# Attention in a three-attention transformer kernel: keys projected before queries, first loads over two queues, first weighings of a half one score item earlier, row group of the maxima by place in the stream

## The reference

```python
x = x + time_mix(layernorm(x))                  # 64x64 state per head, chunks of 64 tokens
x = x + ffn(layernorm(x))                       # "F"
x = x + latent_attention(layernorm(x))          # "L", causal
x = x + ffn(layernorm(x))                       # "H", the same weights as F

def ffn(x):
    h = layernorm(x, ln1_g, ln1_b)
    scores = einsum('bqhd,bkhd->bhqk', h @ Wq, h @ Wk) / sqrt(8)
    x = x + (softmax(scores) @ (h @ Wv)) @ Wo
    m = layernorm(x, ln2_g, ln2_b)
    return x + weighted sum over the 2 best of 8 experts e of gelu(m @ W1[e] + b1[e]) @ W2[e] + b2[e]
```

## Time and profile before

| | |
|---|---|
| time, median of 3 runs | 3130.23 us (3124.28 to 3133.2) |
| profiled execution: its own time | 3137.23 us |
| its span | 3134.4 us |
| PE (TensorE matmul) busy | 2739.7 us, 87% |
| DVE (VectorE) busy | 2117.2 us, 68% |
| ACT (ScalarE) busy | 1712.2 us, 55% |
| POOL (GpSimd) busy | 429.1 us, 14% |
| L543, reduction of the maxima, x2688 | 626.2 + 625.7 + 354.5 us |
| L482, exponentials, x1408 | 522.4 + 522.3 + 294.3 us |

### The profile page before, as it was taken

The page is one execution under the profiler, slowest core; times in us unless marked ns, Lnnn a source line. Parts: engine busy times, 40 slices in busy tenths (PEclk is TensorE's granted clock), DMA queues, the critical chain, the costliest instruction groups (busy, mean ns, idle before and its releaser), DMA issues. The chain is left out here.

```text
span 3134.4 us, 62592 instructions
## 1 busy us (share of the span) xinstructions
PE 2739.7 (87%) x20985; PEld 1214.1 (39%) x20985; DVE 2117.2 (68%) x4017; ACT 1712.2 (55%) x2055; POOL 429.1 (14%) x664
## 2 busy tenths in 40 slices
PE   6788857999999997999599999948998989897998
PEld 2688851223233232444244444421232323233443
DVE  5544456999989895222578777747998989894222
ACT  4222212777777775443156665633776767675433
POOL 1222202111111110000221111120111111110000
PEclk9888856999999998999699999976999999998999
DMA  1000002011100110210201111111110111011111
GB/s 44 1 0 0 0 1 87 23 36 39 39 30 30 39 39 22 82 46 34 87 27 52 53 45 54 47 57 48 39 38 21 39 39 36 23 39 35 69 60 33
DMA packets 86864, 120.25 MB, mean 38 GB/s; under 512 B 16261, under 2 KB 59231, under 8 KB 84223
## 3 DMA queue, kind: packets, MB, share of 16 engines
q1 hardware_dynamic: 83401, 114.80, 11.7%
q10 hardware_dynamic: 3248, 2.21, 0.3%
HBM read 83.40 MB, written 20.55 MB: 33 GB/s over the span
## 5 line engine op out<-in xcount | busy, mean ns | idle before, releaser
L543 DVE TENSOR_REDUCE Hmaxes<-Hm 128x1 f32<-128x512 f32 x1024 | 626.2, 684 | 77.0 <-PE Hm L425 77.0
L543 DVE TENSOR_REDUCE Fmaxes<-Fm 128x1 f32<-128x512 f32 x1024 | 625.7, 684 | 66.1 <-PE Fm L425 66.1
L482 ACT ACTIVATE Hprob<-Hs 128x1024 f32<-128x1024 f32 x512 | 522.4, 1026 | 173.1 <-PE Hs L386 138.8
L482 ACT ACTIVATE Fprob<-Fs 128x1024 f32<-128x1024 f32 x512 | 522.3, 1026 | 161.0 <-PE Fs L386 126.2
L543 DVE TENSOR_REDUCE Lmaxes<-Lm 128x1 f32<-128x512 f32 (+3 forms) x640 | 354.5, 606 | 108.4 <-PE Lm L371 54.5
L482 ACT ACTIVATE Lprob<-Ls 128x1024 f32<-128x1024 f32 (+7 forms) x384 | 294.3, 778 | 177.6 <-PE Ls L386 99.5
L425 PE MATMUL Hm<-Hka,Hqa 60*128 60x512 bf16 x1024 | 299.0, 407 | 66.5 <-DVE Hmaxes L543 32.0
L425 PE MATMUL Fm<-Fka,Fqa 60*128 60x512 bf16 x1024 | 298.9, 406 | 54.3 <-DVE Fmaxes L543 30.5
L404 PE MATMUL Ho<-Hprob,Hvh 128*32 128x256 f32 x4096 | 320.4, 397 | 0.3 <-ACT Hprob L482 0.3
L404 PE MATMUL Fo<-Fprob,Fvh 128*32 128x256 f32 x4096 | 319.9, 396 | 0.3 <-ACT Fprob L482 0.3
L386 PE MATMUL Fs<-Fqa,Fka 60*128 60x512 bf16 x1024 | 248.1, 389 | 1.7 <-ACT Fprob L482 1.7
(11 more groups left out here) (430 smaller groups left out, 3290.2 us busy)
## 6 DMA issues: line engine op xcount, KB each, us to landing
FEwb<-FE_weights SPq DMA_DIRECT2D x8, 1024.0 KB, 5.2
HEwb<-HE_weights SPq DMA_DIRECT2D x8, 1024.0 KB, 5.6
Fvh<-Fvstack SPq DMA_DIRECT2D x17, 256.0 KB
Lvh<-Lvstack SPq DMA_DIRECT2D x17, 256.0 KB
Hvh<-Hvstack SPq DMA_DIRECT2D x17, 256.0 KB
FEw<-in_L_ffn_W SPq DMA_DIRECT2D x16, 256.0 KB, 2.9
HEw<-in_L_ffn_W SPq DMA_DIRECT2D x16, 256.0 KB, 2.8
Fqa<-F_qparts SPq DMA_DIRECT2D x34, 96.0 KB
```

What stands on the lines that cost most here:

```text
L482: nc.scalar.activation(prob[:, :, :].rearrange("p k q -> p (k q)")[:, lo:hi], sps[n % 2][:, o:o + hi - lo], ACT.Exp, scale=SCALE).then_inc ...
L543: nc.vector.reduce_max(maxes[:, a, t, half:half + 1], src[:, 0:w], AX.X).then_inc(max_free, 1)
```

## The change

There are four edits, all in `attention`, and so in F, L and H alike.

1. **Order of the projections.** Keys come first, then queries, then values. The split is interleaved: ScalarE takes the high part of the next piece before the middle part of this one, VectorE subtracts for the next piece before it finishes this one, with three `rest` tiles instead of two.
2. **First loads.** SP stores k and loads `ka` of head 0. ScalarE's queue stores q. `qa` of head 0 is loaded after that, row group 0 by SP and row group 1 by ScalarE's queue. `vh` has a semaphore of its own, `v_loaded`, and is loaded at the start of the second block, as is everything of head 1. One of the two fills of `ka` with minus ones goes from GpSimd to VectorE, ahead of its first subtraction.
3. **`KEPT_BACK`** is 3 instead of 4.
4. **Row group of a maxima matmul**: the parity of its place in the stream of maxima and turns (`PLACE`), not that of its block of keys.

```diff
+    v_loaded = [semaphore(nc, heads, f"{name}v_loaded{s}") for s in range(SLOTS)]
+    vh = heads.enter_context(nc.sbuf_tensor(name + "vh", [P, SLOTS, NT * VW], F32))
+    LOADS = 16 * GROUPS * (2 * PARTS + 1)
...
+    def load_v(engine, h, s):
+        engine.dma_start(vh[:, s, :], vstack[:, bass.ds(h, 1), :, :].rearrange("p h t d -> p (h t d)"))\
+            .then_inc(v_loaded[s], 16)
...
-        QK = [(w, b) for w in range(2) for b in range(NB)]
+        KQ = [(w, b) for w in (1, 0) for b in range(NB)]
...
-                for n, (w, b) in enumerate(QK):
-                    cols = slice(b * BANK, (b + 1) * BANK)
+                def take_high(n):
+                    w, b = KQ[n]
                     act.wait_ge(projected, n + 1)
-                    nc.scalar.activation(parts[:, w, 0, cols], ps[n % 4][:, :], ACT.Copy).then_inc(first, 1)
+                    nc.scalar.activation(parts[:, w, 0, b * BANK:(b + 1) * BANK], ps[n % 4][:, :], ACT.Copy)\
+                        .then_inc(high, 1)
+
+                take_high(0)
+                for n, (w, b) in enumerate(KQ):
+                    if n + 1 < len(KQ):
+                        take_high(n + 1)
                     act.wait_ge(second, n + 1)
-                    nc.scalar.activation(parts[:, w, 1, cols], rest[:, n % 2, :], ACT.Copy).then_inc(first, 1)
+                    nc.scalar.activation(parts[:, w, 1, b * BANK:(b + 1) * BANK], rest[:, n % 3, :], ACT.Copy)\
+                        .then_inc(middle, 1)
+                    if n == NB + 2:
+                        act.wait_ge(split, NB + 2)
+                        store(act, 0, 0, q_stored)
+                act.wait_ge(split, 2 * NB)
+                store(act, 0, 1, q_stored)
                 act.wait_ge(ones, 1)
                 for b in range(NB):
-                    act.wait_ge(projected, len(QK) + b + 1)
+                    act.wait_ge(projected, len(KQ) + b + 1)
 
                     nc.scalar.activation(
                         vstack[:, 0:NH, 4 * b:4 * b + 4, 0:DH].rearrange("p h t d -> p t h d"),
-                        ps[(len(QK) + b) % 4][:, :].rearrange("p (t h d) -> p t h d", t=4, h=NH),
+                        ps[(len(KQ) + b) % 4][:, :].rearrange("p (t h d) -> p t h d", t=4, h=NH),
                         ACT.Copy).then_inc(v_read, 1)
+                act.wait_ge(q_stored, 32)
+                load_q(act, 0, 0, groups=(1,))
+                act.wait_ge(v_read, NB)
 
...
-                for r in range(GROUPS):
-                    nc.gpsimd.memset(ka[64 * r:64 * r + 32, :, :], -1.0).then_inc(filled, 1)
-                pool.wait_ge(filled, 2)
+                nc.gpsimd.memset(ka[0:32, :, :], -1.0).then_inc(filled, 1)
+                pool.wait_ge(filled, 1)
                 nc.gpsimd.memset(vstack[:, :, :, :], 1.0).then_inc(ones, 1)
                 nc.gpsimd.memset(topp[:, :, :, :], 0.0).then_inc(filled, 1)
...
-                for n, (w, b) in enumerate(QK):
+                def take_second(n):
+                    w, b = KQ[n]
+                    dve.wait_ge(high, n + 1)
+                    if n >= 3:
+                        dve.wait_ge(split, n - 2)
+                    nc.vector.tensor_tensor(rest[:, n % 3, :], ps[n % 4][:, :], parts[:, w, 0, b * BANK:(b + 1) * BANK],
+                                            ALU.subtract).then_inc(second, 1)
+
+                nc.vector.memset(ka[64:96, :, :], -1.0).then_inc(minus_ones, 1)
+                take_second(0)
+                for n, (w, b) in enumerate(KQ):
                     cols = slice(b * BANK, (b + 1) * BANK)
-                    dve.wait_ge(first, 2 * n + 1)
-                    nc.vector.tensor_tensor(rest[:, n % 2, :], ps[n % 4][:, :], parts[:, w, 0, cols],
-                                            ALU.subtract).then_inc(second, 1)
-                    dve.wait_ge(first, 2 * n + 2)
-                    nc.vector.tensor_tensor(parts[:, w, 2, cols], rest[:, n % 2, :], parts[:, w, 1, cols],
+                    if n + 1 < len(KQ):
+                        take_second(n + 1)
+                    dve.wait_ge(middle, n + 1)
+                    nc.vector.tensor_tensor(parts[:, w, 2, cols], rest[:, n % 3, :], parts[:, w, 1, cols],
                                             ALU.subtract).then_inc(split, 1)
...
                 for half in range(2):
                     sp.wait_ge(split, 2 * half + 2)
-                    store(sp, 0, half, q_stored)
-
+                    store(sp, 1, half, k_stored)
+                sp.wait_ge(k_stored, 32)
+                sp.wait_ge(minus_ones, 1)
+                sp.wait_ge(filled, 1)
+                load_k(sp, 0, 0)
                 sp.wait_ge(q_stored, 32)
-                load_q(sp, 0, 0)
-                sp.wait_ge(split, NB + 2)
-                store(sp, 1, 0, k_stored)
-                load_q(sp, 1, 1)
-                sp.wait_ge(split, 2 * NB)
-                store(sp, 1, 1, k_stored)
-                sp.wait_ge(k_stored, 32)
+                load_q(sp, 0, 0, groups=(0,))
                 sp.wait_ge(padded, 32)
...
-    KEPT_BACK = 4
+    KEPT_BACK = 3
...
-                for h in range(2):
-                    load_kv(sp, h, h)
+                load_v(sp, 0, 0)
+                load_q(sp, 1, 1)
+                load_k(sp, 1, 1)
+                load_v(sp, 1, 1)
...
-                def weigh(h, s, a, kt):
-
+                def weigh(h, s, a, kt, round_):
+
+                    if a == 0 and kt == 0:
+                        pe.wait_ge(v_loaded[s], (round_ + 1) * 16)
                     pe.wait_ge(expd, 3 + h * NS + a * NSCORE[0] + LAST_ITEM[a][kt])
                     if kt == 0:
...
-                    r = kb % GROUPS
+                    r = PLACE[a, j] % GROUPS
```

More of the change, by code:

```diff
@@ L142, in attention @@
         parts = sb("parts", [P, 2, PARTS, T], BF16)
-        rest = sb("rest", [P, 2, BANK], F32)
+        rest = sb("rest", [P, 3, BANK], F32)
         ps = [ctx.enter_context(nc.psum_tensor(f"{name}pp{i}", [P, BANK], F32)) for i in range(4)]
-        projected, split, first, second, q_stored, k_stored, padded, v_read, ones, filled = (
-            sem(x) for x in ("projected", "split", "first", "second", "q_stored", "k_stored", "padded", "v_read",
-                             "ones", "filled"))
-        QK = [(w, b) for w in range(2) for b in range(NB)]
+        projected, split, high, middle, second, q_stored, k_stored, padded, v_read, ones, minus_ones, filled = (
+            sem(x) for x in ("projected", "split", "high", "middle", "second", "q_stored", "k_stored", "padded", "v_read",
+                             "ones", "minus_ones", "filled"))
+        KQ = [(w, b) for w in (1, 0) for b in range(NB)]
         def store(engine, w, half, stored):
@@ L165, in _ @@
                 for b in range(NB):
-                    n = len(QK) + b
+                    n = len(KQ) + b
                     pe.wait_ge(split, n - 3)
@@ L344, in head @@
                         load_q(sp, h + 2, (u + 2) % SLOTS)
-                        load_kv(sp, h + 2, (u + 2) % SLOTS)
+                        load_k(sp, h + 2, (u + 2) % SLOTS)
+                        load_v(sp, h + 2, (u + 2) % SLOTS)
                     if not first and not causal:
@@ L358, in _ @@
                 sp.wait_ge(loaded[NH % SLOTS], (NH // SLOTS + 1) * LOADS)
+                sp.wait_ge(v_loaded[NH % SLOTS], (NH // SLOTS + 1) * 16)
                 sp.wait_ge(kept, 16 + (NH - 1) * 16)
```

29 lines of the change are left out of this document (13 added, 16 removed).

## The result

The changed kernel took 3102.22 us (median of 4 runs, 3096.98 to 3105.67), the kernel before, run beside it, 3131.46. The ratio is 0.991, 95% interval 0.9886 to 0.9933: faster by 0.9%, where 2.6% was predicted. The profiled execution has a span of 3096.7 us against 3134.4, so 37.7 us have to be found, of 81.0 forecast.

A forecast was written before the change was run, and what follows sets the result against it. VectorE was taken to bound heads of F and H, TensorE those of L, neither the first blocks. 27.4 + 30.7 + 12.5 + 10.4 = 81.0 us off 3137.2 gives 3056.2; less 7.0 for the median, 3049 us, range 3024 to 3084.

The forecast's parts named there:

- the slower rival: Half starts: the granted TensorE clock falls; at all 96 it would cost 187 us, ending at 3236; chance 0.03.
- term 2: KEPT_BACK in F and H: VectorE idles 0.48 us less at each of 64 half starts, 30.7 us in all.
- Term 1: Start of each attention: first maxima 9.1 us earlier, three times, 27.4 us; bounds 21 to 33.
- the rival that the two exclude each other: Attention starts: VectorE's fill waits for GpSimd's, 5.2 us later, three times, ending at 3065; chance 0.06.
- the nearly free fill: Attention starts: a fast mode hides VectorE's fill under 1.8 us, 4.2 us more a start, ending at 3036; chance 0.05.
- The estimate of 6.4 us: VectorE's fill at attention starts: one cycle per element at 0.96 GHz; the forecast itself took 6.0 us.
- Terms 3 and 4: In L: KEPT_BACK gains 12.5 us (bounds 0 and 15.4), row groups of the maxima 10.4 (0 and 21).
- The range of +-15 us: Whole kernel: the forecast's own range around 3049 us, with the bounds of the terms added by squares.
- the order of loads: Attention starts, a sign for the forecast: k loads on SP come before q loads.
- 0.22 us at the half start: Heads, a sign for the forecast: VectorE's idle time at a half start falls from 0.65 to near 0.2 us.
- More stretches at a low clock: Whole kernel: one of the listed signs that would show the prediction wrong; no size given.

The follow-up runs named there:

- after: The changed kernel with all four edits, against the kernel before the change: 3102.22 us, ratio 0.991.
- kb3_alone: The kernel before the change with one edit, KEPT_BACK 3 instead of 4: 3124.17 us, ratio 0.9984 with an interval that holds 1.
- no_groups: The changed kernel with the row group of a maxima matmul taken from its block of keys again (kb % GROUPS): 3105.09 us, ratio 0.9913.
- poolfill: The changed kernel with the second fill of minus ones moved from VectorE back to GpSimd: 3089.07 us, ratio 0.9857.
- before: The kernel without the change, run beside the changed one: 3131.46 us.
- kb4: The changed kernel with KEPT_BACK 4 again, so new starts and row groups alone: 3106.15 us, ratio 0.9917.
- slow2: The changed kernel with five useless VectorE fills of 240 words a head of F and H, in busy stretches: 3099.19 us, ratio 0.9899.
- Pad: The changed kernel with repeated score and maxima matmuls filling TensorE's pause at the division in F and H: 3072.02 us, ratio 0.98.

## Why the prediction was wrong

**The step that failed** is the slower rival, and with it the gain of term 2. I wrote: "Against it: the change fills waits of TensorE, it adds none", gave it 0.03, and let the 30.7 us of term 2 stand as if the granted clock would not change. The argument fails in two places. TensorE does wait longer than before at 8 divisions, for late sums, since the chain of loads on SP did not get shorter with the half. And where the pause is unchanged, falls are more frequent. I had looked at one fall (861.50), asked how long it was, and not how many there are, what comes ahead of each, and whether their number depends on the length of a head. The runs show that it does: 13 to 17 falls at 41.77 us with the pause left as it was (after, kb3_alone, no_groups, poolfill), 1 to 7 at 42.6 (before, kb4, slow2). Pad, which takes them away, gives 30 us back. The mechanism of term 2 was right (0.65 to 0.22 us, 0.43 a half, 27.5 us of 30.7), its gain was 4.1. My rival put the fall at the half start, but it was the division.

**Term 1**, 27.4 forecast, measured 18.4; here the mechanism held and sizes were off. In times from the block's start in F: ScalarE's and VectorE's pieces came as worked out (last piece of k at 12.7 where 12.0 was forecast, last of q at 18.2, 17.6). The first maxima at 497.13 are at the forecast's number by luck, as the block began 3.6 us earlier: 29.6 us in, and 25.8 was forecast. Of the 3.8 us 0.6 are in the last piece of q and the rest on the queues:

```profile
477.41 3.28 SPq L158 DMA_DIRECT2D F_kparts<-Fparts  x2
483.84 5.45 SPq L136 DMA_DIRECT2D Fka<-F_kparts  x6
490.86 1.92 SPq L127 DMA_DIRECT2D Fqa<-F_qparts  x3
...
485.76 0.39 ACTq L158 DMA_DIRECT2D F_qparts<-Fparts  x1
...
490.86 2.87 ACTq L127 DMA_DIRECT2D Fqa<-F_qparts  x3
493.77 0.31 ACTq L129 DMA_DIRECT2D Fqa<-zero_rows  x1
```

The wait for the last store of q was 490.86 - 485.76 = 5.1, not 4.0. ScalarE's four loads took 3.2, not 2.3. From their end to the first maxima it was 497.13 - 494.08 = 3.05, not 1.86. That makes 0.6 + 1.1 + 0.9 + 1.2 = 3.8. I had priced each from rows in which one queue worked alone; that the second queue makes the difference is not shown apart. The loads of k took 5.45 us to issue, with ScalarE's stores beside them, where 3.87 did before, but they ended at 489.3, ahead of the wait, and cost nothing.

The fill was sized near enough, and is what poolfill takes back:

```profile
468.90 5.18 DVE L230 MEMSET Fka<- 32x6144 bf16 x1 [2.98 <-issue]
474.11 1.29 DVE L227 TENSOR_TENSOR Frest<-Fpp,Fparts 128x512 f32<-128x512 f32 x2
```

It ran beside GpSimd's fill of 5.21 us (from 467.55), so the rival that the two exclude each other is out, and so is the nearly free fill. The first agrees with the Trainium skill ("SBUF — State Buffer", section "Who interferes with whom"). The estimate of 6.4 us from "VectorE: DVE Perf Modes", section "Zero memsets can be issued as uint32 (trn2)", of the Trainium skill is longer than the 5.18 of the row. The trace does not settle it: the row begins 1.35 us behind GpSimd's fill in all three attentions, with nothing that VectorE waits for, and the first subtraction starts 474.11 - 467.55 = 6.6 us behind it, where the prediction had 6.0.

**Terms 3 and 4**, 12.5 + 10.4 in L, measured 12.7 from the first maxima to the last weighing. Neither term alone: 503.2 us became 498.0 with the kept-back tile alone (kb3_alone) and 498.6 with the row groups alone (kb4); together 490.6. The 1.42 us of the earlier trace rows was VectorE's, and L is bound by TensorE, so it was no measure of the gain; a head's TensorE work went from 28.21 to 27.41 us, while its idle time rose from 0.76 to 1.05.

**The range of +-15 us** does not follow from the bounds. Towards a smaller gain they are 6, 30.7, 12.5 and 10.4, by squares 35.

**Right:** faster, the order of loads, 0.22 us at the half start, 41.77 for a head (41.7 forecast). "More stretches at a low clock" stood among the signs that would show it wrong, and did.

## What to carry to other kernels

When one engine bounds a loop and TensorE has a pause in it, count the falls of the granted clock in the trace before and look at what stands ahead of each, before you price a few tenths of a us a turn: here a head that was 0.86 us shorter met 17 instead of 6 and gave all of it back. Look also at what runs beside the shortened stretch and was only just in time: here a load that had to land 17.9 us after its chain began now had 17.5. Filling the pause with useful or even repeated matmuls was worth more (pad: 30 us) than the edit under study (KEPT_BACK 3 alone: 7 us, with an interval that holds none), and then the edit was worth 31 us. Price a store, issue or landing that moves beside another queue's traffic above its price alone: here six loads took 5.45 us to issue instead of 3.87, and a store 5.1 to land where 4.0 was forecast.
